# First stage of a two-layer conditioned FFN: the first loads cut smaller and issued in another order

## What is computed

```python
base = einsum('btd,od->bto', x, W)                 # W: 512 x 512
logits = einsum('btd,ed->bte', x, Wr) + 5 * one_hot(language_id)   # 8 experts
gates = softmax over the top 2 of logits
h = einsum('btd,erd->bter', x, A)                  # A: 8 experts x 16 = 128 rows of 512
y = base + 2 * einsum('bter,bte,eor->bto', h, gates, B)
x = x + FFN0(y)     # 4-bit weights, expanded on the chip
x = x + FFN1(cond1(x))
```

## Time and profile before

| | us |
|---|---|
| median of 3 runs (444.40 to 444.64) | 444.44 |
| span of the profiled execution, first to last instruction | 442.5 |
| TensorE busy in the span | 438.1 |
| first product on real data starts | 5.34 |

### The profile page before, as it was taken

One profiled execution on the slowest core, in us unless ns is written; L12 is line 12 of the kernel. 1 busy time (PEld: TensorE's weight loads), 2 busy tenths in 40 slices (PEclk: granted clock), 3 DMA queues, 4 the chain that ended last, 5 costly groups with the idle time before them and its releaser, 6 DMA issues.

```text
span 442.5 us, 5522 instructions
## 1 busy us (share of the span) xinstructions
PE 438.1 (99%) x1954; PEld 358.9 (81%) x1954; DVE 345.7 (78%) x446; ACT 218.7 (49%) x285; POOL 191.2 (43%) x162
## 2 busy tenths in 40 slices
PE   8999999999999999999999999999999999999997
PEld 4688888888888888888888888888888888888886
DVE  4778999798777978947777668868788678999922
ACT  4416466656542213437677656466466554474200
POOL 0457888886017202800005778896987300000000
PEclk9999999999999999999999999999999999999999
DMA  8965022200008694386279527947669146986623
GB/s 283 221 208 159 23 71 80 86 27 1 1 10 275 199 352 194 143 321 250 97 259 329 219 53 233 320 142 225 214 202 285 62 138 262 346 291 181 217 106 142
DMA packets 30456, 79.98 MB, mean 181 GB/s; under 512 B 2384, under 2 KB 15840, under 8 KB 28768
## 3 DMA queue, kind: packets, MB, share of 16 engines
q1 hardware_dynamic: 26752, 68.24, 45.1%
q0 software_dynamic: 3104, 10.73, 8.0%
q10 hardware_dynamic: 576, 0.72, 0.5%
HBM read 58.95 MB, written 20.72 MB: 180 GB/s over the span
## 4 chain that ended last, share of the span: by engine, by line
PE 98%; DMA 1%; DVE 0%; issue 0%; DVEq 0%
PE ps L1935 10%; PE ps L1934 10%; PE ps L1933 10%; PE ps L1670 10%; PE ps L1671 10%; PE ps L1674 10%; PE ps L2047 5%; PE ps L2048 5%; PE ps L1794 5%; PE ps L1793 5%; PE ps L2046 5%; PE ps L1795 5%; PE ps L1916 2%; PE ps L1914 2%; PE ps L1915 2%; DMA res<-in_xT 1%
## 5 line engine op out<-in xcount | busy, mean ns | idle before, releaser
L1670 PE MATMUL ps<-h_hi,ring_hi 128*128 128x512 f32 x152 | 59.1, 389 | 0.0
L1671 PE MATMUL ps<-h_lo,ring_hi 128*128 128x512 f32 x152 | 59.1, 389 | 0.0
L1110 DVE TENSOR_TENSOR ring_lo<-raw,ring_hi 128x1792 fp32r<-128x1792 f32 (+3 forms) x24 | 46.5, 1943 | 11.6 <-ACT ring_hi L746 9.4
L1933 PE MATMUL ps<-zt_hi,ring_hi 128*128 128x512 f32 x140 | 54.6, 390 | 0.0
L1935 PE MATMUL ps<-zt_hi,ring_lo 128*128 128x512 f32 x140 | 54.5, 389 | 0.0
L1934 PE MATMUL ps<-zt_lo,ring_hi 128*128 128x512 f32 x140 | 54.5, 389 | 0.0
L1674 PE MATMUL ps<-h_hi,ring_lo 128*128 128x512 f32 x152 | 47.7, 389 | 0.0
L746 ACT ACTIVATE ring_hi<-raw 128x1792 fp32r<-128x1792 f32 (+1 forms) x23 | 36.6, 1593 | 21.1 <-PE ps L1935 10.1
L636 POOL DMA_INDIRECT scale<-in_sc_gu,idx_gu x20 | 25.6, 1280 | 21.7 <-DVE idx_dn L1147 15.9
L1670 PEld LDWEIGHTS ps<-h_hi,ring_hi 128*128 128x128 f32 x152 | 28.5, 188 | 6.0
L1671 PEld LDWEIGHTS ps<-h_lo,ring_hi 128*128 128x128 f32 x152 | 28.5, 188 | 5.9
(11 more groups left out here) (252 smaller groups left out, 1120.8 us busy)
## 6 DMA issues: line engine op xcount, KB each, us to landing
ad_raw<-in_w1T SPq DMA_DIRECT2D x8, 1024.0 KB, 5.7
wd<-down_weights SPq DMA_DIRECT2D x7, 1024.0 KB, 5.5
down_weights<-dhi SPq DMA_DIRECT2D x7, 896.0 KB, 4.5
down_weights<-dlo SPq DMA_DIRECT2D x7, 896.0 KB, 4.1
raw<-in_gu SPq DMA_DIRECT2D x12, 512.0 KB, 3.6
wd<-down_weights SPq DMA_DIRECT2D x7, 768.0 KB, 5.5
draw<-in_d SPq DMA_DIRECT2D x7, 512.0 KB, 4.7
dn_work<-in_qw_dn SPq DMA_DIRECT2D x11, 256.0 KB
```

The lines of the kernel that those rows point to most:

```text
L1110: dve.tensor_tensor(dst, src, hi_part.bitcast(F32), ALU.subtract).then_inc(done_sem, 1)
L1670: pe.matmul(ps[:, bank + hf, :], w_hi, v_hi[:, t], start=first, stop=False)
L1671: pe.matmul(ps[:, bank + hf, :], w_hi, v_lo[:, t], start=False, stop=False)
L1933: pe.matmul(ps[:, bank, :], ring1_hi[s][:, w], z_hi[:, t], start=first and k == 0, stop=False, skip_group_check=True)
```

## The change

x0's first half becomes two transfers of 256 columns. The 128 columns of A for slice 0 get a transfer of their own (64 KB), the rest of aw0 (144 KB) follows in a second one. ScalarE alone makes hi of x0, now in three instructions, and VectorE makes hi and lo of A's first columns before anything of the rest of aw0. TensorE does tile 0 of the first 512 tokens in two groups of 256 columns, each with three products, and tiles 1 and 2 after both. The warm-up has 6 matmuls in place of 8. aw2, aw3 and cst are issued by ScalarE behind hi of aw1 in place of at the warm-up's ticks.

```diff
-        X_PIECES = [(0, slice(0, HALF)), (0, slice(HALF, T))] + [(k, slice(0, T)) for k in range(1, KD)]
+        X_PIECES = [(0, slice(0, HALF // 2)), (0, slice(HALF // 2, HALF)), (0, slice(HALF, T))] + [(k, slice(0, T)) for k in range(1, KD)]
...
@@ SyncE
-            load_x(0)
-            load_x(1)
+            for i in range(3):
+                load_x(i)
             sp.dma_start(aw_raw[:, aw_cols(1)], a["aw"][:, aw_cols(1)]).then_inc(s_aw[1], 16)
-            for i in range(2, len(X_PIECES)):
+            for i in range(3, len(X_PIECES)):
...
@@ ScalarE
-            load_aw(0)
+            act.dma_start(aw_raw[:, 0:P], a["aw"][:, 0:P]).then_inc(s_awa, 16)
+            act.dma_start(aw_raw[:, P:aw_cols(0).stop], a["aw"][:, P:aw_cols(0).stop]).then_inc(s_aw[0], 16)
             act.wait_ge(s_warm, 1)
             act.activation(col[:, 0:1], zn_dn[:, 0:1], ACT.Copy)
-            act.wait_ge(s_tick, 3)
-            load_aw(2)
-            act.wait_ge(s_tick, 4)
-            load_aw(3)
-            act.wait_ge(s_tick, 5)
-            act.dma_start(cst[:, :], a["cst"]).then_inc(s_cst, 16)
...
-            for i in range(2, NX):
+            for i in range(3, NX):
                 if X_SPLITS[i][2].start == 0:
                     aw_hi_part(X_SPLITS[i][1])
+                if i == 3:
+                    load_aw(2)
+                    load_aw(3)
+                    act.dma_start(cst[:, :], a["cst"]).then_inc(s_cst, 16)
                 x_hi(i)
...
@@ VectorE
-            dve.wait_ge(s_x[0], 16)
-            dve.tensor_copy(act_hi[:, 0, x0_rest], res[:, 0, x0_rest]).then_inc(s_dhi, 1)
+            dve.wait_ge(s_awa, 16)
+            dve.tensor_copy(aw_hi[:, 0, 0:P], aw_piece(0)[:, 0:P]).then_inc(s_first, 1)
+            x_lo(0)
+            dve.wait_ge(s_first, 1)
+            lo(aw_lo[:, 0, 0:P], aw_piece(0)[:, 0:P], aw_hi[:, 0, 0:P], s_first)
             dve.wait_ge(s_aw[0], 16)
-            dve.tensor_copy(aw_hi[:, 0, 0:P], aw_piece(0)[:, 0:P]).then_inc(s_dhi, 1)
-            dve.tensor_copy(aw_hi[:, 0, P:3 * P], aw_piece(0)[:, P:3 * P]).then_inc(s_dhi, 1)
-            dve.wait_ge(s_dhi, 3)
-            x_lo(0)
-            aw_lo_part(0)
+            dve.tensor_copy(aw_hi[:, 0, P:3 * P], aw_piece(0)[:, P:3 * P]).then_inc(s_first, 1)
             x_lo(1)
+            dve.wait_ge(s_first, 3)
+            lo(aw_lo[:, 0, P:3 * P], aw_piece(0)[:, P:3 * P], aw_hi[:, 0, P:3 * P], s_wlo0)
+            x_lo(2)
...
@@ TensorE
-            for _ in range(8):
-                pe.matmul(ps[:, 0, :], warm[:, 0:P], warm, start=True, stop=True).then_inc(s_tick, 1)
+            for _ in range(6):
+                pe.matmul(ps[:, 0, :], warm[:, 0:P], warm, start=True, stop=True)
             pe.wait_ge(s_x[0], 16)
-            pe.matmul(ps[:, 0, :], warm[:, 0:P], warm, start=True, stop=True)
+            pe.matmul(ps[:, 6, :], warm[:, 0:P], warm, start=True, stop=False)
...
+            for i, (_, c) in enumerate(X_PIECES[0:2]):
+                pe.wait_ge(s_xhi, i + 1)
+                pe.wait_ge(s_first, 1)
+                pe.matmul(ps[:, 6, c], aw_hi[:, 0, 0:P], act_hi[:, 0, c], start=False, stop=False, skip_group_check=True)
+                pe.wait_ge(s_xlo, i + 1)
+                pe.matmul(ps[:, 6, c], aw_hi[:, 0, 0:P], act_lo[:, 0, c], start=False, stop=False, skip_group_check=True)
+                pe.wait_ge(s_first, 2)
+                pe.matmul(ps[:, 6, c], aw_lo[:, 0, 0:P], act_hi[:, 0, c], start=False, stop=False, skip_group_check=True)
             for hf in range(NH):
                 th = slice(HALF * hf, HALF * hf + HALF)
-                pe.wait_ge(s_xhi, hf + 1)
-                for j, bank in enumerate((6, 0, 4)):
-                    pe.wait_ge(s_dhi, min(j, 1) + 2)
+                tiles = ((1, 0), (2, 4)) if hf == 0 else ((0, 6), (1, 0), (2, 4))
+                pe.wait_ge(s_xhi, hf + 2)
+                pe.wait_ge(s_first, 3)
+                for j, bank in tiles:
                     pe.matmul(ps[:, bank + hf, :], aw_hi[:, 0, P * j:P * j + P], act_hi[:, 0, th], start=True, stop=False)
```

More of the change, by code:

```diff
@@ L256, in build @@
         ps = ctx.enter_context(nc.psum_tensor("ps", [P, 8, HALF], F32))
-        X_PIECES = [(0, slice(0, HALF)), (0, slice(HALF, T))] + [(k, slice(0, T)) for k in range(1, KD)]
-        X_SPLITS = [(0, 0, slice(0, HALF)), (1, 0, slice(HALF, T))] + [
-            (k + 1, k, slice(HALF * hf, HALF * hf + HALF)) for k in range(1, KD) for hf in range(NH)]
+        X_PIECES = [(0, slice(0, HALF // 2)), (0, slice(HALF // 2, HALF)), (0, slice(HALF, T))] + [(k, slice(0, T)) for k in range(1, KD)]
+        X_SPLITS = [(i, k, t) for i, (k, t) in enumerate(X_PIECES[0:3])] + [
+            (k + 2, k, slice(HALF * hf, HALF * hf + HALF)) for k in range(1, KD) for hf in range(NH)]
         NX = len(X_SPLITS)
@@ L750, in x_hi @@
                 act.wait_ge(s_x[piece], 16)
-                if i == 0:
-                    t = slice(0, HALF // 2)
                 hi(act_hi[:, k, t], res[:, k, t], s_xhi)
@@ L757, in aw_hi_part @@
                 hi(aw_hi[:, k, :], aw_piece(k), s_whi0)
-            x_hi(0)
-            x_hi(1)
+            for i in range(3):
+                x_hi(i)
             act.wait_ge(s_aw[0], 16)
             hi(wr2[:, :, 0:E], wr[:, :, :], s_wrhi)
-            for i in range(2, NX):
+            for i in range(3, NX):
                 if X_SPLITS[i][2].start == 0:
                     aw_hi_part(X_SPLITS[i][1])
+                if i == 3:
+                    load_aw(2)
+                    load_aw(3)
+                    act.dma_start(cst[:, :], a["cst"]).then_inc(s_cst, 16)
                 x_hi(i)
@@ L1120, in aw_lo_part @@
                 lo(aw_lo[:, k, :], aw_piece(k), aw_hi[:, k, :], s_wlo0)
-            x0_rest = slice(HALF // 2, HALF)
-            dve.wait_ge(s_x[0], 16)
-            dve.tensor_copy(act_hi[:, 0, x0_rest], res[:, 0, x0_rest]).then_inc(s_dhi, 1)
-            dve.wait_ge(s_aw[0], 16)
-            dve.tensor_copy(aw_hi[:, 0, 0:P], aw_piece(0)[:, 0:P]).then_inc(s_dhi, 1)
-            dve.tensor_copy(aw_hi[:, 0, P:3 * P], aw_piece(0)[:, P:3 * P]).then_inc(s_dhi, 1)
-            dve.wait_ge(s_dhi, 3)
-            x_lo(0)
-            aw_lo_part(0)
+            dve.wait_ge(s_awa, 16)
[3 more added lines that the diff above has]
+            lo(aw_lo[:, 0, 0:P], aw_piece(0)[:, 0:P], aw_hi[:, 0, 0:P], s_first)
+            dve.wait_ge(s_aw[0], 16)
+            dve.tensor_copy(aw_hi[:, 0, P:3 * P], aw_piece(0)[:, P:3 * P]).then_inc(s_first, 1)
             x_lo(1)
+            dve.wait_ge(s_first, 3)
+            lo(aw_lo[:, 0, P:3 * P], aw_piece(0)[:, P:3 * P], aw_hi[:, 0, P:3 * P], s_wlo0)
+            x_lo(2)
             dve.wait_ge(s_wrhi, 1)
             lo(wr2[:, :, E:2 * E], wr[:, :, :], wr2[:, :, 0:E], s_wrlo)
-            for i in range(2, NX):
+            for i in range(3, NX):
                 if X_SPLITS[i][2].start == 0:
@@ L1705, in router @@
                 return ins
+            for i, (_, c) in enumerate(X_PIECES[0:2]):
[6 more added lines that the diff above has]
+                pe.matmul(ps[:, 6, c], aw_lo[:, 0, 0:P], act_hi[:, 0, c], start=False, stop=False, skip_group_check=True)
             for hf in range(NH):
                 th = slice(HALF * hf, HALF * hf + HALF)
-                pe.wait_ge(s_xhi, hf + 1)
-                for j, bank in enumerate((6, 0, 4)):
-                    pe.wait_ge(s_dhi, min(j, 1) + 2)
+                tiles = ((1, 0), (2, 4)) if hf == 0 else ((0, 6), (1, 0), (2, 4))
+                pe.wait_ge(s_xhi, hf + 2)
+                pe.wait_ge(s_first, 3)
+                for j, bank in tiles:
                     pe.matmul(ps[:, bank + hf, :], aw_hi[:, 0, P * j:P * j + P], act_hi[:, 0, th], start=True, stop=False)
-                pe.wait_ge(s_xlo, hf + 1)
-                for j, bank in enumerate((6, 0, 4)):
+                pe.wait_ge(s_xlo, hf + 2)
+                for j, bank in tiles:
                     pe.matmul(ps[:, bank + hf, :], aw_hi[:, 0, P * j:P * j + P], act_lo[:, 0, th], start=False, stop=False)
                 pe.wait_ge(s_wlo0, 1)
-                for j, bank in enumerate((6, 0, 4)):
+                for j, bank in tiles:
                     pe.matmul(ps[:, bank + hf, :], aw_lo[:, 0, P * j:P * j + P], act_hi[:, 0, th], start=False, stop=False)
```

4 lines of the change are left out of this document (2 added, 2 removed).

## The result

The changed kernel is slower: 458.36 us, median of 4 runs (458.15 to 459.40), against 444.42 for the kernel before on the same chip (4 runs, 444.18 to 444.64). The ratio is 1.0315, its 95% interval 1.0303 to 1.0328. The prediction was 445.1 with a range of 444.0 to 446.3, so it missed by 13.3 us. The profiled execution's span went from 442.5 to 456.4, 13.9 more.

A forecast was written before the change was run, and what follows sets the result against it. TensorE, busy 99% of the span, was taken to bound the kernel. Head 0.0, stall at the transposes 0.7 and rest nothing took the span from 442.5 to 443.2; plus 1.9 gave 445.1 us, range 444.0 to 446.3.

The forecast's parts named there:

- I take 7.0 for aw3: Moved loads: aw3, issued at 7.1, takes 7.0 us and lands at 14.1; range of landings 11.3 to 14.7.
- a stall of 0.6 at slice 2: Slice 2's first product: aw2 lands at 13.0, needs 1.9 us more, 14.9 against 14.30; counted inside the 0.7 stall.
- the log copy: Transposes: the copy ends at 21.4, TensorE wants it at 20.7, a stall of 0.7; generally aw3's landing less 13.4.
- Rival 2: Moved loads land later than 14.7, with nib's 1.4 MB in front; aw3 at 16 gives +2.6, 447.0; chance 0.11.
- a stall of 1.9: Upper end of the forecast range: a stall of 1.9 us, giving 446.3.
- GpSimd's gathers "at nothing": Gathers behind the index arithmetic start up to 2 us later, covered by the rest of the projection: cost nothing.
- The warm-up "at nothing": Six warm-up matmuls in place of eight: the clock's rise may fall into a pause of about 0.5 us; cost nothing.
- The head "0.0": Slice 0: x's first 256 columns land at L = 4.3, second half of the tokens starts at 7.65, change 0.0.
- the lower bound of 3.91: Head: earliest landing of x's first 256 columns, counted by bytes alone; L = 3.91 gives a change of -0.38.
- L + 1.59: Head: VectorE's last lo of the first half ends 1.59 us after the landing L of x's first 256 columns.
- 1.77: Head: TensorE's products between VectorE's last lo and the start of the second half of the tokens take 1.77 us.
- The moved loads' issue: ScalarE, behind hi of aw1: aw2 issued at 6.7, aw3 at 7.1, cst at 7.5, about 4 us later than before.

The follow-up runs named there:

- e3: Changed kernel, with SyncE issuing the two nib loads only when cst has landed: 450.46 us median, ratio 1.0072 to the kernel before.
- e2: Kernel before with only the issue of aw2, aw3 and cst moved behind hi of aw1: 455.74 us, ratio 1.0262.
- f1: Changed kernel, with GpSimd waiting for the gates' product before its second set of scale gathers: 452.95 us, ratio 1.0177 to the kernel before.
- f4: Kernel before with only GpSimd's wait for the gates' product before its second set of gathers: 444.48 us, ratio 0.9998.
- e1: Changed kernel with aw2, aw3 and cst issued at warm-up ticks again, still 6 warm-ups: 446.37 us median, ratio 1.0056 to the kernel before.
- e4: Changed kernel with aw2, aw3 and cst issued behind hi of x0's second 256 columns: 448.98 us median, scattered, ratio 1.0121 to the kernel before.
- f3: Kernel before with 6 warm-up matmuls in place of 8, nothing else: 445.93 us in two groups, ratio 1.0017.
- g3: Changed kernel with aw2, aw3 and cst at warm-up ticks and 8 warm-ups: 445.20 us, ratio 1.0012 to the kernel before.
- g2: Changed kernel with aw2, aw3 and cst at warm-up ticks, 6 warm-ups, GpSimd's second gathers waiting for the gates' product: 445.82 us, ratio 1.0030 to the kernel before.
- g1: Changed kernel with aw2, aw3 and cst at warm-up ticks, 8 warm-ups, GpSimd's second gathers waiting for the gates' product: 445.42 us, ratio 1.0017 to the kernel before.

## Why the prediction was wrong

**The failed step** is "I take 7.0 for aw3" with the upper end at 7.6. It measured 13.6, and aw2 9.2 where 6.3 stood, cst 14.6 where 9.0 did. I took the nearest rows for the moved loads from transfers that had been issued at 2.7 us, ahead of nib, and applied them to an issue right behind it (nib at 7.04, aw2 at 7.33), with the argument that "nothing is ahead of them in ScalarE's own queue". e3 shows the size of that error: without nib in flight aw3 takes 7.0. Having a queue of one's own did not help. The Trainium skill has a rule for this (DMA: Bandwidth & Descriptors, "Queues, rings and completion order"): both engines' queues are served by the same 16 DMA engines, each of which takes its queues in turn, one packet at a time. The trace agrees. The DMA view counts packets, MB and share of the 16 engines for each queue (q1 is SyncE's, q10 ScalarE's). First the kernel after from 7.4 to 11 us, then from 14 to 19:

```profile
q1 hardware_dynamic: 377, 1.18, 100.1%
```

```profile
q1 hardware_dynamic: 144, 1.00, 89.9%
q10 hardware_dynamic: 143, 0.16, 16.1%
```

From 7.4 to 11 us nothing of ScalarE's queue moves, and the same is so in e3. From 14 to 19 the turns are equal, 144 to 143, but the bytes are not: SyncE's packets have 6.9 KB on average and take 0.50 us each (the share, times 5 us, times 16 engines, over the count), ScalarE's 1.1 KB and 0.09 us. By these counts each small packet of the moved loads comes behind a large one of nib's queue. In e3, from 11 to 15 us, ScalarE's queue moves 0.50 MB beside 0.52.

**The consequence that I dropped.** With aw2 at 13.0 I found a stall of 0.6 at slice 2 that "isn't added". With the real landing at 16.54 the same sum (1.9 from landing to product) gives 18.44, which is the measured start. That it fits to the hundredth is luck, since the three terms of the 1.9 add up to 1.83. The mechanism was right and its input wrong by 3.5 us. Likewise the log copy: landing of aw3 less 13.4 would have given 7.95; the lag at the fifth transpose is 7.80.

**Rival 2 was the case** (0.11). It named nib's 1.4 MB, and put "aw3 at 16" as its example, +2.6; at 21.35 its own formula gives 8. The range stopped at a stall of 1.9. The upper bound should have come from bytes: what is queued ahead at the issue, over the rate of the stretch.

**The fallen clock behind a stall** was not in any stall's price. Three steps of 0.55 to 1.9 us, 4.2 in all, came on top behind two stalls: there TensorE went on at 1.2 GHz. In the window 20.4 to 24.0 the granted clock is 0.50, after an idle stretch of 3.73. The Trainium skill states it (TensorE: Matmul & The Clock Gate, "HAM oscillation — how this bites in real kernels": a wait for a DMA inside a kernel brings the slow clock back) and this trace agrees. It doesn't happen every time: e2 has the same idle time at the gates' product, 3.73 us, and goes on at a granted clock of 1.00.

**GpSimd's gathers "at nothing".** I asked only who waits for them, not what they meet when they shift. The second set came 5.98 us later (30.63 to 36.61), the transposes 7.81 (29.30 to 37.11), and so an order that had held by 0.3 us turned round. The late signal cost 3.9 us at TensorE, and 1.7 of clock behind that. In f1's trace, with the gathers held back, both are gone, and f4 shows that holding them back is free. But e1, e4, f3 and g3 have the turned order without the delay, so the order is not the whole cause, and how a signal of TensorE's is held up is open.

**The warm-up "at nothing".** Wrong by about 0.4 us (g2 against g1) to 1.0 (e1 against g3, each less its own kernel before) and 1.5 in the medians of f3 and its kernel before, as a matter of luck from run to run. The prediction counted on a pause between warm-up and first x; x landed at 3.53, before the sixth warm-up was through, and there was none.

**The head "0.0"** was 0.2 off, and as near as that by luck, since its errors cancel. The landing was 3.53, better than the lower bound of 3.91. The chain behind it held: the last lo was put at L + 1.59 and ended at 5.17, L + 1.64. From there the second half was to start 1.77 later, 6.94; it started at 7.86, the 0.92 between being the slow clock. With 8 warm-ups and the loads back at the ticks (g3) the 1.77 holds (5.67 to 7.45), but the lo ends 0.5 later, since ScalarE issues cst from 3.56 on before it makes the first hi. What then took the 0.20 away was x's slice 1, moved back by one issue on SyncE's queue: I counted that issue for x0 and aw1 and not for x1. The choice to compare at the second half's start was an error of its own. In e3 that start comes 0.74 sooner and slice 1 only 0.06, since slice 1 then waits for its x.

**The moved loads' issue** was put at 6.7 and was 7.33, since aw1, now at 2.16, took 5.1.

## What to carry to other kernels

Price a moved load by what is in flight at its new place: bytes issued ahead of it on every queue, over the rate that this stretch shows. The time that it took at its old place is no bound. Worked from the kernel before, this gives a fair estimate of the latest landing: up to and with aw3 5.1 MB are issued, and by 20.4 us that kernel had moved its bytes at 261 GB/s, so 5.1 MB are through at an estimated 19.7 us. aw3 landed at 21.35, aw2 well before, at 16.54. Look at the packets too: a load in small ones, sharing the engines turn by turn with one in large ones, gets few of the bytes. Where a stall on TensorE is found, put the slow clock behind it into the range (here 0 to 2.5 us for a stall), and follow what shifts on the engines beside it until something meets: here late loads shifted the index arithmetic, a set of gathers came to lie ahead of a signal, and with it the signal came late, which cost 4 us, 17 us behind the load's landing. When an early transfer is split, look at the last one in that queue that is wanted just in time.

## What the runs showed of the hardware

- The same 192 KB load took 7.6 us issued at 3.1, 9.1 at 4.6, 11.6 at 6.7, 13.6 at 7.7 and 15.3 at 8.1 (aw3 in the kernel before, e4, e2, the kernel after, f1), and 7.0 issued at 7.9 with nib held back (e3).
- With packets of two queues in flight the engines gave both equal turns (144 and 143 from 14 to 19 us in the kernel after) and unequal bytes (1.00 and 0.16 MB).
- A 128 KB load with nothing ahead of it in its queue landed in 2.8 us, and beside it a 64 KB one on the other queue in 3.0; 256 KB beside 208 KB had taken 3.98.
- A signal of TensorE's reached VectorE 3.8 to 5.3 us late in three traces where GpSimd had begun the second set of indirect gathers before it (e2, e3, the kernel after). In four more with this order it came within 0.04 (e1, f3, g3) and 0.35 us (e4), and within 0.04 in all seven where the set began later. Why is not settled; a single gather moved alone, or the set with another destination, was not tried.
- 6 warm-up matmuls in place of 8 gave the kernel before two groups of runs, 444.1 to 444.4 and 445.8 to 447.6, and the profiled one of the upper group has the clock at 1.2 GHz over slice 0. With 8, slice 0 began at 1.2 GHz in g1 and at 2.4 GHz in g3.
- Behind 3.7 to 3.8 us of idle time at the same place TensorE went on at a granted clock of 0.57 in one trace (the kernel after) and of 1.00 in another (e2).
